# Band attention: which engine begins the builds of queries, keys and values

## The reference

```
q, k, v = (x @ Wq + bq), (x @ Wk + bk), (x @ Wv + bv)     # 16 heads of 16
scores = q k^T / 4, masked to |i - j| <= half             # half <= 60, from the data
attn = softmax(scores);  out = attn v;  out = out W_o;  return out @ Wfc + bfc
```

## Time and profile before

| | us |
|---|---|
| median of 3 executions | 4360.22 |
| their range | 4354.43 to 4363.12 |
| the profiled execution's own time | 4360.39 |
| its span, first to last instruction | 4358.7 |

### The profile page before, as it was taken

The page is one execution under the profiler, slowest core; times in us unless marked ns, Lnnn a source line. Parts: engine busy times, 40 slices in busy tenths (PEclk is TensorE's granted clock), DMA queues, the critical chain, the costliest instruction groups (busy, mean ns, idle before and its releaser), DMA issues. The chain is left out here.

```text
span 4358.7 us, 47735 instructions
## 1 busy us (share of the span) xinstructions
PE 3492.9 (80%) x16943; PEld 1763.7 (40%) x16943; DVE 2423.3 (56%) x4118; ACT 1683.0 (39%) x2694; POOL 1125.9 (26%) x967
## 2 busy tenths in 40 slices
PE   6889989876589999998997998412992688778799
PEld 2333444333233333333332655301661355456465
DVE  2999999999277676676771233672003133344212
ACT  4655555553135555455554121200220234333322
POOL 3766677765220012210000000002003422211000
PEclk9999999999799999999998999555996888889899
DMA  2222222221411211211201000002222655653100
GB/s 77 71 68 68 60 75 71 68 66 53 75 40 21 36 29 36 42 33 28 33 9 45 15 10 5 1 0 87 87 92 58 122 100 108 105 92 60 30 20 20
DMA packets 205940, 230.84 MB, mean 53 GB/s; under 512 B 57912, under 2 KB 155529, under 8 KB 204413
## 3 DMA queue, kind: packets, MB, share of 16 engines
q1 hardware_dynamic: 201502, 215.45, 21.6%
q0 software_dynamic: 4224, 12.59, 0.9%
HBM read 182.07 MB, written 45.88 MB: 52 GB/s over the span
## 5 line engine op out<-in xcount | busy, mean ns | idle before, releaser
L1363 DVE TENSOR_REDUCE g_mxp<-PS 128x1 f32<-128x512 f32 (+3 forms) x1280 | 723.0, 606 | 219.3 <-PE PS L1509 119.6
L1235 ACT ACTIVATE g_pT<-PS 128x1024 f32<-128x1024 f32 (+3 forms) x640 | 552.7, 894 | 476.2 <-PE PS L1524 282.4
L377 POOL TENSOR_TENSOR WB<-m_dtx,WB 128x1024 f32<-128x1024 f32 x256 | 601.6, 2354 | 297.0 <-DVE WB L521 269.7
L409 ACT ACTIVATE PS<-m_dt,m_A 128x512 f32<-128x512 f32 x512 | 353.3, 691 | 437.0 <-DVE WB L512 436.5
L1501 PE MATMUL PS<-g_KT,WB 96*128 96x512 bf16 (+3 forms) x1280 | 425.8, 360 | 105.9 <-DVE g_mxp L1363 93.0
L606 PE MATMUL PS<-WB,ident 128*128 128x512 f32 x1024 | 503.7, 615 | 0.0
L512 DVE TENSOR_TENSOR_SCAN WB<-PS,m_state,WB 128x512 f32<-128x512 f32 x384 | 471.1, 1269 | 14.9 <-ACT PS L409 14.8
L1524 PE MATMUL PS<-WB,g_KT 99*128 99x512 bf16 (+3 forms) x1280 | 358.2, 352 | 1.2 <-ACT g_pT L1235 0.6
L521 DVE TENSOR_TENSOR WB<-WB,PS 128x1024 f32<-128x1024 f32 x256 | 307.8, 1202 | 9.9 <-PE PS L592 4.2
L1501 PEld LDWEIGHTS PS<-g_KT,WB 96*128 96x128 bf16 x1280 | 116.4, 98 | 479.3 <-DVE g_mxp L1363 399.8
L1543 PE MATMUL PS<-g_pT,WA 128*32 128x512 f32 (+3 forms) x2560 | 301.9, 544 | 0.6 <-ACT g_pT L1235 0.6
(11 more groups left out here) (294 smaller groups left out, 5380.0 us busy)
## 6 DMA issues: line engine op xcount, KB each, us to landing
WB<-b_rows SPq DMA_DIRECT2D x256, 256.0 KB, 3.1
WB<-in_L_ffn_w SPq DMA_DIRECT2D x18, 1024.0 KB, 8.6
WB<-g_dq SPq DMA_DIRECT2D x96, 128.0 KB, 4.0
WB<-w_dq SPq DMA_DIRECT2D x96, 128.0 KB, 7.4
w_KT<-w_dk SPq DMA_DIRECT2D x96, 128.0 KB, 7.9
g_rden<-g_dn SPq DMA_DIRECT2D x128, 64.0 KB, 2.0
w_dv<-WA SPq DMA_DIRECT2D x8, 1024.0 KB, 5.6
w_V<-w_dv SPq DMA_DIRECT2D x16, 512.0 KB, 11.4
```

What stands on the lines that cost most here:

```text
L377: pool.tensor_tensor(hh[:, g % RING, :, :], dtx[:, MB * h:MB * h + MB, :], Bs[:, g % BRING, :].unsqueeze(1) .broadcast_to([P, MB, CH]), AL ...
L409: act.activation(PS[:, 2 + b, :], dt[:, c % 2, m, :], ACT.Exp, scale=Aneg[:, n, m:m + 1]).then_inc(dA_ready, 1)
L1235: act.activation(pT[:, n % 2, 2 * pair:2 * pair + 2, 0:width], PS[:, 2 * pair:2 * pair + 2, at:at + width], ACT.Exp, scale=DH ** -0.5).the ...
L1363: dve.tensor_reduce(mxp[:, q % 6, i % QB, hh:hh + per, k0 // CH if causal else 0], PS[:, 4 + m % 2, :].rearrange("p (h n) -> p h n", h=per ...
```

## The change

Three edits:

1. The body of the build, until now in SP's walk through the list, becomes a function `build(eng, u)` with the same waits and the same 13 transfers.
2. SP calls it in the causal attention alone; in band attention ACT calls it at the build's place in its own walk. All other transfers stay with SP.
3. In band attention the build's place in the list moves back by one window (`+ 1`).

```diff
--- before.py
+++ after.py
@@ -793,7 +793,7 @@
         for u in range(NS * NJ):
             c = u % NJ
             need.append(began[2 * u] if causal or c == 0 else reached[2 * (u - 1)])
-            acts.append((need[u] - build_lead, "build", u))
+            acts.append((need[u] - build_lead + (0 if causal else 1), "build", u))
         end = float("inf")
         parts = ("q0", "r0", "q1", "r1", "k", "v") if causal else ("q0", "q1", "k0", "k1", "v0", "v1")
         prepared = []
@@ -978,6 +978,36 @@
             t = TPB * (s // 2) + QB * J + 2 * r
             return slice(t, t + 2)
 
+        def build(eng, u):
+
+            s, c = u // NJ, u % NJ
+            b, half = s // 2, s % 2
+            for kind in (f"q{half}", "k" if causal else f"k{half}"):
+                it = item(kind, b, c)
+                eng.wait_ge(stored[it % slots], 16 * (it // slots + 1))
+            eng.wait_ge(v_stored, 16 * (NJ * b + c + 1))
+            if u >= QRING:
+                w = u - QRING
+                if causal or c == NJ - 1:
+                    eng.wait_ge(pv, first[2 * w + 2])
+                else:
+                    eng.wait_ge(pv, first[2 * w + 3] + 1)
+            for j, (qp, kp) in enumerate(PAIRS):
+                rows = slice(DH * j, DH * j + DH)
+                cells = slice(CH * c, CH * c + CH)
+                eng.dma_start(QT[rows, u % QRING, :, :],
+                             dq[b, qp, P * half:P * half + P, cells]
+                             .rearrange("(h d) t -> d h t", d=DH))\
+                    .then_inc(built[u % QRING], 16)
+                n = nk * DH
+                eng.dma_start(KT[rows, region(s, c), :, :],
+                             dk[b, kp, n * half:n * half + n, cells]
+                             .rearrange("(h d) t -> d h t", d=DH))\
+                    .then_inc(built[u % QRING], 16)
+            eng.dma_start(V[:, region(s, c), :, :, :],
+                         dv[b, c, :, :, nk * half:nk * half + nk, :])\
+                .then_inc(built[u % QRING], 16)
+
         with nc.Block() as block:
             @block.sync
             def _(sp):
@@ -1051,35 +1081,8 @@
                         b, c = x
                         sp.wait_ge(w_free, use["v" if causal else "v1", b, c] + 1)
                         sp.dma_start(dv[b, c], Vst[:, :, :, :]).then_inc(v_stored, 16)
-                    elif what == "build":
-                        u, = x
-                        s, c = u // NJ, u % NJ
-                        b, half = s // 2, s % 2
-                        for kind in (f"q{half}", "k" if causal else f"k{half}"):
-                            it = item(kind, b, c)
-                            sp.wait_ge(stored[it % slots], 16 * (it // slots + 1))
-                        sp.wait_ge(v_stored, 16 * (NJ * b + c + 1))
-                        if u >= QRING:
-                            w = u - QRING
-                            if causal or c == NJ - 1:
-                                sp.wait_ge(pv, first[2 * w + 2])
-                            else:
-                                sp.wait_ge(pv, first[2 * w + 3] + 1)
-                        for j, (qp, kp) in enumerate(PAIRS):
-                            rows = slice(DH * j, DH * j + DH)
-                            cells = slice(CH * c, CH * c + CH)
-                            sp.dma_start(QT[rows, u % QRING, :, :],
-                                         dq[b, qp, P * half:P * half + P, cells]
-                                         .rearrange("(h d) t -> d h t", d=DH))\
-                                .then_inc(built[u % QRING], 16)
-                            n = nk * DH
-                            sp.dma_start(KT[rows, region(s, c), :, :],
-                                         dk[b, kp, n * half:n * half + n, cells]
-                                         .rearrange("(h d) t -> d h t", d=DH))\
-                                .then_inc(built[u % QRING], 16)
-                        sp.dma_start(V[:, region(s, c), :, :, :],
-                                     dv[b, c, :, :, nk * half:nk * half + nk, :])\
-                            .then_inc(built[u % QRING], 16)
+                    elif what == "build" and causal:
+                        build(sp, *x)
                     elif what == "use" and x[0] == "rows":
                         q = x[1]
                         s, J, g = block_of(q)
@@ -1244,6 +1247,8 @@
                                 act.wait_ge(normed, q - ORING + 1)
                             act.activation(Ot[:, q % ORING, :], PS[:, 6, :], ACT.Copy)\
                                 .then_inc(o_out, 1)
+                    elif what == "build" and not causal:
+                        build(act, *x)
                     elif what == "part0":
                         it, = x
                         n = item_rows(it)
```

## The result

| | us |
|---|---|
| median after, 15 executions | 4344.69 (4327.93 to 4352.78) |
| median before, 15 executions | 4356.77 (4342.98 to 4372.03) |
| ratio of the two | 0.997, 95% interval 0.9957 to 0.9982 |
| profiled execution after: time, span | 4352.78, 4351.0 |

A forecast was written before the change was run, and what follows sets the result against it. PE sets the pace, with waits for small transfers queued behind builds. Removing 101.1 us of waits, against 69 for ACT's stops and 1 + 3.5 + 3 + 4, gives -20.6 us: 4340 us, range 4304 to 4395.

The forecast's parts named there:

- The stalls that go: Band attention, 3440 to 4056 us: PE's waits for `WB<-w_dm` (63.7 us) and `w_On` (37.4) all go, -101.1 us.
- ACT's stops: At 13 builds, 3 to 15, ACT issues for 6.9 us and delays PE by 5.3 us: +69 us.
- my own sign for the mechanism: Unit 6's rows load should be issued within 3 us of its store and land within 4 us.
- Why they go: SP no longer holds 13 issues ahead of each small transfer, and begins these when their data are there.
- Rival 3: ACT issues slowly, 11.4 us per build, each costing 4.5 us more: 58 us, so 4398 us; chance 0.20.
- Rival 4: ACT issues at the low bound, 4.3 us per build, 2.6 less: 34 us, so 4306 us; chance 0.13.
- The first three builds: In the preparation of chunks 2 and 3: +1 us for builds 0 and 1, +3.5 us for build 2.
- Late builds: Builds issued about 1 window (2 to 3 us) later land late, pair 12 and 13 tightest: +3 us.
- The clock: After PE's stalls the clock is slow for a while; shorter stops leave more of that to work: +4 us.
- The sum: Whole kernel: -101.1 + 69 + 1 + 3.5 + 3 + 4 = -20.6 us, so 4340 us.
- Rival 2: Small transfers still queue behind the build's data; `w_On` waits keep 16 us: 4356 us, no change; chance 0.17.

The follow-up runs named there:

- e2_act_only: The changed kernel without the third edit: ACT begins the builds, at their old place in the list; 4331.06 us, ratio 0.9949.
- e1_window_only: The kernel before with the third edit alone: builds stay with SP, their place one window later; 4314.53 us, ratio 0.9901.
- e6_rows_pool: The changed kernel, but GpSimd begins the rows store and rows load, through its software queue; 4347.22 us, one execution.

## Why the prediction was right, and where not

**The stalls that go.** The direction was right, and so was the balance of two large sums, 101 us off against ACT's stops. But I let all 101.1 us go, and 18 stayed (w_On 12.0, w_dm 6.0). I had tested it at unit 6 with small transfers of a few us; the store there took 10.6 us. That PE did not wait for these rows was luck: the slack of 15 us, which I had counted for two transfers of a few us, was just enough for 13.4 (the load's packets run from 3596.4 to 3596.9). PE comes to the rows at 3604.04, and without ACT's stop of 5.49 us just before it would have been 3598.6. Of my own sign for the mechanism the first half (the load issued within 3 us of its store) failed; the second held (landed within 4 us), since the load is issued only 1.1 us after build 5's first issue. Unit 22, with build 12 ahead of its store and build 13 behind, waited 5.97 us.

**Why they go** was half wrong. I wrote that what this removes is 13 issues in front of each small transfer, and priced the extra window at nothing but later builds. `e2_act_only` shows that moving the builds off SP is worth 27 us alone; `e1_window_only` shows that the window alone puts the rows loads of units 8, 16 and 24 ahead of builds 6, 10 and 14 (no rows wait there, against 7.2, 9.6 and 11.4 us) and is worth 43. This was to be read from the list of acts, in which SP's `build 6` stood just ahead of `rows_in 8`. Weighing a change of three edits as one sum, I never asked what each would do alone.

**ACT's stops** were well sized: 5.3 us at 13 builds, 69 us, against 65 measured (3.0 to 6.3 each, mean 5.0). The nearest row, SP's own issues, was the right price: 6.2 to 8.4 us per build on ACT too. Rival 3 needed 8.5 us at every build. Rival 4 fell: an issue on ACT takes 0.45 us.

**The first three builds.** Stops of 6.7, 3.2 and 4.8 us came in the preparation, and the waits for builds 0 and 1 (7.5 and 6.0 us) almost vanished for it. From the stage's first product to the first `turn` it took 120.4 us, before 121.0. I had -1.8 (1 + 3.5 - 6.3).

**Late builds**: +3 expected, none measured beyond 2.9 us in all, less than before; PE, later by ACT's stops, came after them.

**The clock** was about right. Between the first `turn` and the last output the half-speed level was granted for 108 us instead of 137, but what costs is PE's work in it, and that was 79.5 us instead of 76.4: the shorter stops leave more of each slow stretch to work, as the forecast said. After ACT's stop at 3601.05, for one, it lasted to 3607.4. PE's busy time over the whole stretch rose by 2.5 us, against +4.

**The sum** by stretches: from the first `turn` to the last output 573.9 us before and 559.4 after, -14.5, of which PE's idle time is -17.0 and its busy time +2.5. With -0.6 in the preparation this is -15.1 against the forecast's -20.6. The terms that were off: +18.0 for stalls that stayed, -3.6 for ACT's stops, +1.2 for the preparation, -3.7 for late builds, -1.5 for the clock, and -3.2 for a `w_On` wait at 4056.81, just behind the window of the earlier trace rows. With these the forecast is -13.4; 1.7 us stay open. The largest mis-sized term is the 101.1, of which 83.1 went.

**Rival 2** lies between. A small transfer issued behind most of a build does land with it, where the forecast let all pass, and the `w_On` waits kept 12.0 us; but one issued in the first us passes all but a few pieces (4.4 to 4.6 us), and the gain of 12 us by the medians is half way between the rival's 4 and the forecast's 20. The rival's 16 us did not follow from its own words either: of eight waits of 37.4 us in all, the trace has two longer than 5.3 us (8.18 and 11.02), which leaves 8.6.

The Trainium skill, DMA: Bandwidth & Descriptors, "Issuing engines are not separate DMA queues", says that transfers run on the same 16 DMA engines and interleave whoever begins them. The trace agrees that a second issuer gives no free way past a build (10.6 us beside 1.4); for the 9.4 us between the store's issue and the next packet of SP's queue, at 3592.9, it shows no interleaving. "Queues, rings and completion order" on the same page, by which each DMA engine serves its rings in turn, did not help this transfer. The same page of the Trainium skill, "Back-pressure in remote DMA", says of transfers between cores that stalled writes hold the source engine's other queues too; within one core the packet counts above and `e6_rows_pool` (10.1 us) look like that, but no run here shows that this is the cause.

## What to carry to other kernels

Moving transfers to a compute engine's queue costs their issue time there, 0.48 us apiece, whenever that engine feeds the bound one with less slack than that; count the slack at the place (0.67 us at build 3), not the engine's mean load of 38%. Before moving work between queues, try to reorder and spread it in the queue where it is: put the urgent small transfers ahead, begin large ones when their buffers are free, and cut them so that none stands behind more than one piece. And take a change of several edits apart before pricing it, since edits that remove the same wait don't add up.

## What the runs showed of the hardware that I had not expected

- A small transfer was held by how much of a build had been issued ahead of it, though in another queue. Behind 13 issues it took 10.6 us (a 12 KB store in SP's hardware queue beside ACT's) and 10.1 us (in GpSimd's software queue), 1.4 us without a build in flight; an 8 KB store took 4.4 to 4.6 us when it was issued 0.6 us after the build's first.
- A build whose neighbouring transfers write the same 16 partitions was slower than one whose neighbours write different ones (and read the parts of `w_dk` in another order): 146 against 132 ns per 1 KB packet, 18.5 against 16.2 us per build, 21 us of the kernel's time.
- An issue costs ACT what it costs SP: 0.45 us, 0.48 with the gap to the next.
